# Graph attention on one core: a ninth block of sixteen turned by DMA instead of TensorE

## The reference

```
h = maximum(layernorm(x), 0)                  # x: 8192 x 128, fp32
scores = leaky_relu(h @ ks.T, 0.2)            # 8192 x 8192
scores = where(adj > 0, scores, -9e15)        # adj: 8192 x 8192, int32
attn = softmax(scores, axis=1)
out = x + attn @ ks
```

## Time and profile before

| what | value |
|---|---|
| median of 3 runs | 1658.87 us (1658.17 to 1659.25) |
| the profiled execution | 1658.6 us, its span 1656.8 us |
| TensorE busy (weight loads apart) | 1609.1 us, 97% (1181.7, 71%) |
| VectorE | 1491.6 us, 90% |
| ScalarE | 1400.4 us, 85% |
| GpSimd | 1155.8 us, 70% |
| DMA packets | 641340, 417.78 MB, mean 252 GB/s |
| time of the packets of the one hardware queue, share of 16 engines' span | 103.9% |
| granted TensorE clock, mean | 0.995 |
| chain that ended last | PE 70%, DVE 18%, issue 4%, ACT 2%, POOL 1% |

### The profile page before, as it was taken

The page is one execution under the profiler, slowest core; times in us unless marked ns, Lnnn a source line. Parts: engine busy times, 40 slices in busy tenths (PEclk is TensorE's granted clock), DMA queues, the critical chain, the costliest instruction groups (busy, mean ns, idle before and its releaser), DMA issues.

```text
span 1656.8 us, 38135 instructions
## 1 busy us (share of the span) xinstructions
PE 1609.1 (97%) x13442; PEld 1181.7 (71%) x13442; DVE 1491.6 (90%) x2592; ACT 1400.4 (85%) x2081; POOL 1155.8 (70%) x1224
## 2 busy tenths in 40 slices
PE   5699999999999999999999999999999999999999
PEld 3477777777777777777777777777777777777777
DVE  7999899899899899999999999999998998998996
ACT  6688888888888888888888888888888888888887
POOL 1576776776776767767767767767767767767766
PEclk8999999999999999999999999999999999999999
DMA  7799999999999999999999999999999999999996
GB/s 235 196 230 261 253 264 256 248 265 269 249 263 254 254 262 263 253 261 255 254 265 259 253 260 253 264 266 248 262 260 256 263 262 248 268 258 244 272 253 127
DMA packets 641340, 417.78 MB, mean 252 GB/s; under 512 B 551040, under 2 KB 575616, under 8 KB 641152
## 3 DMA queue, kind: packets, MB, share of 16 engines
q1 hardware_dynamic: 641152, 415.34, 103.9%
HBM read 276.82 MB, written 4.19 MB: 170 GB/s over the span
## 4 chain that ended last, share of the span: by engine, by line
PE 70%; DVE 18%; issue 4%; ACT 2%; POOL 1%; DMA 0%; DVEq 0%; POOLq 0%
PE ps_out L386 20%; PE ps_T L371 10%; PE ps_out L387 10%; PE ps_scores L360 10%; PE ps_scores L362 10%; PE ps_scores L361 10%; DVE mask L573 8%; DVE scores L591 5%; DVE probsT_lo L600 2%; ACT probsT_hi L470 2%; DVE hT_hi L516 1%; DVE row_min L606 1%; DVE plain_max L609 1%; POOL keys_in L314 0%; PE ps_out L338 0%
## 5 line engine op out<-in xcount | busy, mean ns | idle before, releaser
L314 POOL TENSOR_TENSOR keys_in<-scores,keys_in 128x512 f16<-128x512 f32 x512 | 652.2, 1274 | 41.4
L591 DVE CUSTOM_DVE_ANT_0 scores<-ps_scores,mask,minus_scale 128x1024 f32<-128x1024 f32 x512 | 652.8, 1275 | 1.4 <-PE ps_scores L362 0.6
L312 POOL CAST keys_in<-scores 128x512 f16<-128x512 f32 x512 | 346.0, 676 | 402.3 <-ACT scores L462 402.0
L462 ACT ACTIVATE scores<-scores,neg_max 128x1024 f32<-128x1024 f32 x512 | 582.5, 1138 | 0.0
L453 ACT ACTIVATE scores<-scores 128x1024 f32<-128x1024 f32 x512 | 537.8, 1050 | 51.9 <-DVE pair_min L591 51.8
L600 DVE TENSOR_TENSOR probsT_lo<-ps_T,probsT_hi 128x512 f16<-128x512 f32 x512 | 350.2, 684 | 130.1 <-ACT probsT_hi L470 130.1
L470 ACT ACTIVATE probsT_hi<-ps_T 128x512 f16<-128x512 f32 x512 | 305.7, 597 | 186.1 <-PE ps_T L371 185.7
L386 PE MATMUL ps_out<-keys,probsT_hi 128*128 128x256 f16 x2048 | 392.8, 272 | 18.8 <-DVE probsT_lo L600 12.8
L360 PE MATMUL ps_scores<-keysT_hi,hT_hi 128*128 128x512 f16 x1024 | 391.2, 382 | 16.4 <-DVE keysT_lo L555 9.4
L361 PE MATMUL ps_scores<-keysT_lo,hT_hi 128*128 128x512 f16 x1024 | 390.5, 381 | 0.0
L362 PE MATMUL ps_scores<-keysT_hi,hT_lo 128*128 128x512 f16 x1024 | 390.1, 381 | 0.0
(11 more groups left out here) (52 smaller groups left out, 830.0 us busy)
## 6 DMA issues: line engine op xcount, KB each, us to landing
adj_in<-in_adj_dram SPq DMA_DIRECT2D x512, 512.0 KB, 5.1
keys_in<-keys_in SPq DMA_TRANSPOSE x512, 4.9
x_in<-in_x_dram SPq DMA_DIRECT2D x64, 64.0 KB, 2.1
keys_in<-in_L_gnn_ks_dram SPq DMA_DIRECT2D x8, 512.0 KB, 7.3
out_dram<-out_tile SPq DMA_DIRECT2D x64, 64.0 KB, 1.8
```

What stands on the lines that cost most here:

```text
L314: nc.gpsimd.tensor_tensor(half[:, BLOCK:2 * BLOCK], probs(t, b), half[:, 0:BLOCK], ALU.subtract) \
L462: nc.scalar.activation(s, s, ACT.Exp, bias=neg_max[:, t % 2:t % 2 + 1], scale=-SLOPE, accum_out=pair_sum[:, t % 2, p:p + 1]).then_inc(prob ...
L591: nc.vector.tensor_tensor_reduce(out=score_pair(q, p), in0=ps_scores[:, slots, :].rearrange("p s k -> p (s k)"), in1=mask[:, (p // 2) % 2, ...
```

## The change

Block 12, an even one, goes from `BY_PE` to `BY_DMA`: nine of the sixteen blocks are turned by DMA, seven by TensorE. The slots for halves go from four to six and those for turned blocks from six to eight.

```
-    R_SLOTS = 4
+    R_SLOTS = 6
     X_SLOTS = 4
-    D_SLOTS = 6
+    D_SLOTS = 8
@@
-    BY_DMA = tuple(b for b in range(BLOCKS) if b % 2 == 1)
+    BY_DMA = tuple(b for b in range(BLOCKS) if b % 2 == 1 or b in (12,))
     BY_PE = tuple(b for b in range(BLOCKS) if b not in BY_DMA)
```

## The result

The changed kernel takes 1652.95 us (median of 7 runs; the kernel before 1658.62 beside it). One of the seven took 2754.91 us at a granted clock of 0.556, and the ratio is taken from the other six. Its profiled execution took 1652.08 us, the span is 1650.3 us.

What follows compares the result with a forecast made beforehand. TensorE was taken as the bound, the DMA engines a close second; the slower of 24.40 and 24.6 us a tile saves 0.43 over 62 tiles: 1658.6 - 26.7 + 1.8 = 1633.7, rounded to 1633 us, range 1611 to 1675.

Steps and rivals of the forecast that it cites:

- TensorE's side: Turn of a tile: turning (0.43 us) and wait for block 12's low part (0.36) go, a 0.16 us wait appears.
- The step that failed is GpSimd's: Block 12's added split on GpSimd, 1.77 us a tile: meeting VectorE's masks priced at 0, at most 0.86 us.
- the prediction's own count for TensorE: TensorE's time for a tile: 25.03 - 0.43 - 0.36 + 0.16 = 24.40 us.
- The term of the DMA engines: One added transpose a tile, 0.9 to 2.55 us against 1.18 us idle; tile taken as 24.6 us.
- 1621: Rival: TensorE remains the bound and the DMA engines keep up at 24.40 us a tile; 1621 us, chance 0.27.
- The rival that came true: Gain swallowed by DMA need or a wait moved to the first pair's masking: 25.0 us a tile, 1655 to 1662, chance 0.11.
- sign that SP's waits for GpSimd would fall: On SP's queue: waits for GpSimd's splits should fall from 6.5 us a tile to 4 or less.
- the 261 GB/s: Skill's effective DMA transpose rate: 1.00 us for 262 KB, giving 24.85 us a tile and about 1649 us in all.
- The slower rival: Added transpose needs over 1.18 us on the DMA engines, TensorE waits for turned blocks: 1693 to 1745 us, chance 0.22.
- The slots: More slots for halves and turned blocks keep earlier splits from waiting for block 12's transpose, and cost nothing.
- The end of the run: Last tile: GpSimd splits back to back, so a ninth split adds 1.8 us to the run.

Runs made afterwards that it cites:

- block 11's move: Changed kernel with turned block 11 added in slot 3 instead of slot 5: 1620.73 us, ratio 0.9777; the same in the kernel before: 1658.63 us, ratio 1.0.
- ten blocks: Changed kernel with block 4 also turned by DMA (ten of sixteen) and block 11 added in slot 3: 1724.47 us, ratio 1.0392.

## Why the prediction was wrong

*TensorE's side was right.* The turning (0.43 us) and the wait for block 12's low part (0.36 us) went, block 12's output matmuls moved at the same cost, and the next thing late was, as named, the masking of the first pair. Without GpSimd's second split the wait for it is 0.22 us, where the prediction had 0.16.

*The step that failed is GpSimd's:* "I price it at 0, at most 0.86." I looked for masks that a ninth split might meet and found room on VectorE over the whole tile, 2.3 us. But the second split works exactly beside the chain that the same prediction had made the next bound. It even had the time right: block 15's split would come 0.5 us later. It came 0.42 us later (7.38 us after the tile's store, 6.96 in the kernel before), and this is what puts its copy on `plain_max`, an instruction too small to be looked at. Measured by itself the second split costs 0.43 us a tile, taken away as well as added. The wait came out at 0.65 us instead of 0.16, and with these 0.49 us more the prediction's own count for TensorE gives 24.40 + 0.49 = 24.89 us a tile; it is 24.91. What GpSimd doesn't pay of the 0.49, some 0.06, lies in the step from the mask to the masking, which is also there without the second split (819.47 to 819.59).

*The term of the DMA engines was wrong as well,* in the other direction: 0.9 to 2.55 us a tile against 1.18 us idle. A ninth transpose costs 0.9 us in the whole run, 0.01 us a tile, with the share at 109.8%; I had taken a share above 1 for need. 24.6 us a tile was therefore too much by this term and too little by the other. The wrong term moved the forecast from 1621 to 1633, towards the result, and that was luck. With both put right the sum is 1658.9 - 62 x 0.14 + 1.8 = 1652 us. The rival that came true is the second, a gain swallowed by the first pair's masking, which I had at 0.11 and at 1655 to 1662; its price was a little too high. Its place was right, but not why the wait grows: GpSimd's work stretches the chain.

Two more things in the prediction need an answer. Its sign that SP's waits for GpSimd would fall from 6.5 us a tile to 4 or less did not come: they are 392.7 us in all, 6.1 a tile. And the 261 GB/s that it takes from the Trainium skill ("DMA: Bandwidth & Descriptors", Latency and other measured facts) stand there for a transpose with a non-contiguous middle dimension; for the contiguous case the page has some 350 to 400 GB/s, by which the 262 KB would take 0.66 to 0.75 us, an estimate. The row shows 0.90 us, beside other loads, and the forecast rests on neither figure.

*The slower rival* had its mechanism in the DMA engines and did not come. A slower outcome lay nearby all the same, in TensorE's cover: with block 8 the same edit makes the kernel 1.07% slower. The prediction says of the moved output matmuls that they "cost the same". So they do, but where they stood they hid 0.66 us of another engine's chain. For block 12 the prediction counted that, as it took the 0.66 us off block 4's start; what it did not see is that cover can be brought from elsewhere, which is worth 32 us, as block 11's move shows.

*The slots* cost nothing and bring nothing, as said. The end of the run was right: from the last `row_min` to the end of the span it takes 23.9 us in the kernel before (1632.9 to 1656.8) and 25.5 in the changed one (1624.8 to 1650.3), 1.6 us more where 1.8 was put.

## What to carry to other kernels

When work is taken off the engine that is busy throughout, ask for every piece, removed or moved, which other engine's chain it was covering; a place where the engine waits right behind is worth work from anywhere else. Price an addition on a neighbour engine by what runs beside it on the next bound, not by that engine's idle time over the whole tile. And before a queue with a share above 1 is called full, add one transfer that nobody waits for and see whether the time moves.

## What the runs showed of the hardware

An instruction of VectorE with one number a partition took 0.50 us instead of 0.16 beside GpSimd's copy of 512 columns, in the changed kernel and again where only the split had been added (0.52). It ends when GpSimd's instruction ends: at 804.07, the copy at 804.06, and to within 0.04 us in each of the 52 tiles in the middle of the run. With ten blocks a subtraction of 1.16 us runs beside it instead, and it takes 0.88 us in the middle of the tiles. So its cost is what is left of GpSimd's instruction, and not its own size. GpSimd pays too: the copy at 805.63 (block 1 of the next tile) took 1.22 us beside the mask, and the same copy in the kernel before, with the mask over, 0.61 (810.26). The Trainium skill ("GPSIMD Engine Reference", section 8, Key points) names VectorE's two-port modes and instructions with two SBUF inputs as what contends; `plain_max` has two SBUF inputs, so the trace agrees; the prediction had taken up the two-port modes alone. That a wait of 0.34 us falls on so small an instruction I had not expected. The DMA engines moved 576 transposes of 256 KB instead of 512, beside the same loads, with a landing time 0.3 us longer (5.2 against 4.9).
